# Two weight and activation tiles moved by 64 bytes each in a kernel of 32 graph blocks

## The chip, the cores and the metric

The kernel runs on one core of one Trainium2 chip, as one program in one launch. The metric is the device time of that program in microseconds; the median of three runs of the kernel before is 1295.74 us (1294.81 to 1297.44).

## The reference

32 graphs of 256 nodes with 256 features each (`x`), each with a dense 256 x 256 adjacency `adj`, pass through four blocks, each of them "layernorm of x plus block(x)":

- block 0: `relu(concat(x, adj @ x / deg) @ W.T)`;
- block 1: three graph convolutions, `adj @ (x @ Wi) + bi`, with relu after the first two;
- block 2: attention of 8 heads of 64 over the nodes: `qkv = x @ W_qkv`, `softmax(q @ k.T / 8) * 0.33 + 0.33 * adj + 0.33 * exp(-adj)` times `v`, then `@ W_out + b_out`, with a node mask;
- block 3: `scores = q @ k.T / 8` with a small `q` and `k` (64), a row sum of `scores * adj`, a softmax of that over the nodes, and its product with `x @ W_v.T`.

All of it is float32.

## The kernel before

One graph is one pass through all four blocks, and four or five graphs are in work at once. After a head (`first_graphs`) that fills this pipeline comes a loop of 28 equal slots (`slot(s)`, s from 5 to 32), in which each engine does the steps of graphs s-5 to s+1 in an order written out by hand, and then a tail (`last_graphs`). The order of the TensorE steps of a slot stands at L1834 to L1881.

To get float32 accuracy from the one-pass float32r products, each operand is kept in two tiles, a high part (`_h`) and a low part (`_l`); a product a @ b becomes a_h b_h + a_h b_l + a_l b_h. The helper `product` (L1506) issues these; `nodes_product` (L1532 on) issues a 256 x 256 by 256 x 256 product as 12 matmuls of 128 x 128 by 128 x 256, often cut in 8 that need only the high part of the late operand (`HI`) and 4 that need its low part (`LO`). In each matmul the left argument is the stationary operand, loaded into the array by a LDWEIGHTS of its own, and the right one is the moving operand. The trace names the moving operand first: `psum<-wout_h,oT_h` streams wout_h past the stationary oT_h.

The matmuls of a slot which read float32r tiles of 128 partitions, in their order, are these (moving x stationary tile, count):

- `hidden(0)` sup x w123, 8 then 4, with `tail_adj_k` (k3 x adjT, 8) between;
- four steps of transposes, two of scores, two of attend, `gate_row`;
- `support(1)` w123 x hidT, 12; `qk(2)` x2T x wqkv, 12; `support0 HI` w0 x fT, 8; `hidden(1)` adjT x sup, 12; `support0 LO` w0 x fT, 4; `self_product` w0 x fT, 12; `project_out` wout x oT, 24; `support(2)` w123 x hidT, 12; `values HI` wqkv x x2T, 8 of 512 columns; `gcn_out` sup x adjT, 12; `values LO`, 4 of 512 columns; `aggregate` sup x adjT, 12; `qk(3)` x2T x wqkv, 12;
- `gate_column`, transposes, scores, attend, `x3_transpose`;
- `qk(0)` x2T x wqkv, 12; `tail_project HI` w3 x x3T, 8 of 384 columns; `mix` adjT x fT, 12; `tail_project LO`, 4 of 384 columns; `qk(1)` x2T x wqkv, 12; and then the next slot's `hidden(0)`.

Every tile is a static buffer of each partition, placed by `sb()` right behind the one before it, at the next multiple of 32 bytes. Three unused buffers (`space_0`, `space_1` of 64 bytes, `space_2` of 32) and 16 unused elements in each row of `qkT` (`HALF` is 16 elements, 64 bytes) stand between tiles. With them every product of high and low parts has its two operands 64 bytes apart modulo 128.

What prints below are the function that allocates the tiles and the TensorE steps.

Of the kernel before, what the change touches and what calls it, by code (L numbers as in the profile page):

```python
# [13 lines left out]
def graph_blocks_kernel(nc, x_d, adj_d, nodemask, xT_d, adjT_d, w0_d, w123_d, L1_b1, L1_b2, L1_b3, wqkv_d, wout_d,  # L14
# [3 lines left out]
    P = 128  # L18
# [12 lines left out]
    HALF = 16  # L31
# [5 lines left out]
    with ctx:  # L37
        def sb(name, shape, dt=F32):
            return ctx.enter_context(nc.sbuf_tensor(name, shape, dt))
# [20 lines left out]

        w0 = [sb(f"w0_{s}", [P, FT, 2 * F], F32R) for s in "hl"]
        w123 = [sb(f"w123_{s}", [P, 3, FT, F], F32R) for s in "hl"]
        wqkv = [sb(f"wqkv_{s}", [P, FT, 3, INNER], F32R) for s in "hl"]
        wout = [sb(f"wout_{s}", [P, PAIRS, F], F32R) for s in "hl"]
        w3 = [sb(f"w3_{s}", [P, FT, L3C], F32R) for s in "hl"]

# [29 lines left out]
        x2_pre = sb("x2_pre", [P, NT, F])  # L96
        x2 = sb("x2", [P, NT, F])
        x2_bout = sb("x2_bout", [P, 2, NT, F])
        x2T = [sb(f"x2T_{s}", [P, FT, N], F32R) for s in "hl"]


        v_sb = sb("v_sb", [P, NT, INNER])
        w0_raw = v_sb
        qkT = [sb(f"qkT_{s}", [P, 2, 2, N + HALF], F32R)[:, :, :, 0:N] for s in "hl"]
# [2029 lines left out]
```

How the kernel before makes its waits and increments, by code:

```python
        def reuse(eng, semaphore, n):  # L239
            if n > 0:
                eng.wait_ge(semaphore, n)
# [7 lines left out]
        @block.sync  # L250
# [35 lines left out]
            def store(g):  # L286
                b = g % 2
                sp.wait_ge(act_y, once(g))
                sp.dma_start(out_d[bass.ds(g, 1)].rearrange("g p n f -> (g p) n f"), y_sb[:, b]) \
                    .then_inc(dma_out[b], 16)
# [28 lines left out]
            load_nodes(1)  # L319
            sp.dma_start(wqkv_raw[:, :, :], wqkv_d).then_inc(dma_wqkv, 16)
            sp.dma_start(wout_raw[:, :, :], wout_d).then_inc(dma_wout, 16)
            sp.dma_start(w3_raw[:, :, :], w3_d).then_inc(dma_w3, 16)
            for k in range(2, G + 6):
                if live(k):
                    load(k)
                if live(k - 6):
                    store(k - 6)
            for b in range(2):
                sp.wait_ge(dma_out[b], 16 * (G // 2))
# [1 line left out]
        @block.gpsimd  # L331
        def _(pool):
            nc.gpsimd.memset(one[:, :], 1.0)
            nc.gpsimd.memset(eps[:, :], LN_EPS)
            nc.gpsimd.memset(minus_half[:, :], -0.5).then_inc(pool_const, 1)
            nc.gpsimd.memset(ident[:, :], 0.0).then_inc(pool_ident, 1)
            pool.wait_ge(pool_ident, 1)
            nc.gpsimd.affine_select(out=ident[:, :], in_=ident[:, :], compare_op=ALU.not_equal, fill=1.0,
                                    base=0, pattern=[[-1, P]], channel_multiplier=1).then_inc(pool_ident, 1)
            pool.wait_ge(pool_const, 1)
```

## Time and profile before

| what | value |
|---|---|
| median of 3 runs | 1295.74 us |
| profiled execution, its own time | 1296.16 us |
| its span, first to last instruction | 1294.4 us |
| TensorE matmul busy | 1269.5 us, 98% |
| TensorE weight load busy | 1162.2 us, 90% |
| VectorE busy | 1160.8 us, 90% |
| ScalarE busy | 969.8 us, 75% |
| GpSimd busy | 179.3 us, 14% |
| DMA, mean | 38 GB/s |
| chain that ended last | TensorE 94% |
| granted TensorE clock | 0.998 |

Matmuls overlap, and the end of each is modelled: a row's length (0.28 us for 256 columns) is not what a matmul costs. What it costs is the distance from its start to the start of the next. In the views by time a row with xN is N matmuls of one form, and the second number is the time from the start of the first to the end of the last.

### The profile page before, as it was taken

The page shows a single profiled execution, that of the slowest core. Times are in us where ns is not written, and L with a number is a line of the kernel's source. Part 1 is how long each engine was busy: PE and PEld are TensorE (multiplying, and loading weights), DVE is VectorE, ACT ScalarE, POOL GpSimd, SP SyncE. Part 2 cuts the span into 40 slices and gives each one's busy share as a digit, 9 for nine tenths or more (in the row PEclk, how much of TensorE's full clock was granted, in tenths as well). Part 3 has the DMA queues.
Part 4 walks back from the last instruction along what each step waited for, and adds up shares of the span by engine and source line. Part 5 has one row for each costly group of instructions (what it writes and reads, how often), then busy time and mean ns, then how long its engine had stood idle before and what let it go on. Part 6 is the DMA issues. An engine that isn't in the chain of part 4 may idle for free.

```text
span 1294.4 us, 30393 instructions
## 1 busy us (share of the span) xinstructions
PE 1269.5 (98%) x10848; PEld 1162.2 (90%) x10848; DVE 1160.8 (90%) x3661; ACT 969.8 (75%) x2573; POOL 179.3 (14%) x393
## 2 busy tenths in 40 slices
PE   7999999999999999999999999999999999999996
PEld 7898899999999999999999999999999999999985
DVE  7988999999999999999999999999999999998984
ACT  7677777778778778778778777787777787777773
POOL 0100111101111101111101111101111111111101
PEclk9999999999999999999999999999999999999999
DMA  6110111110111110111110111100111100110000
GB/s 227 34 35 2 35 43 43 44 43 1 43 43 43 43 43 2 43 43 43 43 31 14 43 43 43 43 26 19 43 44 43 43 17 28 43 43 10 10 9 25
DMA packets 34309, 49.02 MB, mean 38 GB/s; under 512 B 7920, under 2 KB 16880, under 8 KB 34160
## 3 DMA queue, kind: packets, MB, share of 16 engines
q1 hardware_dynamic: 34160, 47.08, 11.5%
q8 instruction: 88, 1.44, 0.5%
q14 instruction: 61, 0.50, 0.1%
HBM read 38.68 MB, written 8.39 MB: 36 GB/s over the span
## 4 chain that ended last, share of the span: by engine, by line
PE 94%; ACT 2%; DVE 2%; DMA 1%; POOL 1%; issue 1%; SPq 0%; ACTq 0%; POOLq 0%; DVEq 0%
PE psum L1506 63%; PE psum L1520 11%; PE psum L1756 9%; PE psum L1714 8%; PE psum L1807 1%; PE psum L1810 1%; PE psum L1819 1%; ACT work L545 1%; DMA adjT_sb<-in_adjT 1%; PE psum L1830 0%; ACT x L597 0%; POOL rstd L349 0%; DVE bn L902 0%; DMA v_sb<-in_w 0%; DVE work L1080 0%
## 5 line engine op out<-in xcount | busy, mean ns | idle before, releaser
L545 ACT ACTIVATE work<-work,shift 128x256 f32<-128x256 f32 x512 | 253.2, 498 | 5.5 <-DVE shift L1061 5.5
L1080 DVE SCALAR_TENSOR_TENSOR work<-work,rsum,extra 128x256 f32<-128x256 f32 x512 | 217.0, 475 | 1.0
L396 ACT ACTIVATE work<-psum 128x512 f32<-128x512 f32 x256 | 138.1, 595 | 73.3 <-PE psum L1520 69.4
L1061 DVE CUSTOM_DVE_ANT_0 work<-psum,minus_big 128x256 f32<-128x256 f32 x512 | 189.5, 417 | 3.3 <-PE psum L1714 3.2
L346 POOL TENSOR_TENSOR mv<-mv,eps 128x2 f32<-128x2 f32 x128 | 31.0, 243 | 1094.4 <-DVE mv L923 1094.4
L396 ACT ACTIVATE sup_h<-psum 128x512 fp32r<-128x512 f32 x124 | 73.3, 591 | 117.8 <-PE psum L1506 117.5
L1506 PE MATMUL psum<-x2T_h,wqkv_h 128*128 128x256 f32 x512 | 145.7, 285 | 0.0
L1506 PE MATMUL psum<-x2T_l,wqkv_h 128*128 128x256 f32 x512 | 143.0, 279 | 0.0
L1506 PE MATMUL psum<-x2T_h,wqkv_l 128*128 128x256 f32 x512 | 142.8, 279 | 0.0
L1520 PE MATMUL psum<-ident,work 128*128 128x128 f32 x1024 | 129.0, 274 | 0.0
L1756 PE MATMUL psum<-work,v_sb 128*64 128x256 f32 x1024 | 124.7, 385 | 1.0 <-ACT work L396 1.0
L396 ACT ACTIVATE qkT_h<-psum 128x512 fp32r<-128x512 f32 x128 | 75.3, 589 | 55.9 <-PE psum L1506 55.7
L1520 PEld LDWEIGHTS psum<-ident,work 128*128 128x128 f32 x1024 | 113.0, 141 | 1.4 <-DVE work L1080 0.6
L349 POOL TENSOR_TENSOR rstd<-mv,minus_half 128x2 f32<-128x2 f32 x128 | 106.9, 835 | 10.0
L1756 PEld LDWEIGHTS psum<-work,v_sb 128*64 128x64 f32 x1024 | 67.9, 136 | 37.4 <-ACT work L396 1.4
L873 DVE TENSOR_TENSOR sup_l<-psum,sup_h 128x512 fp32r<-128x512 f32 x124 | 85.0, 686 | 14.4 <-ACT sup_h L396 14.2
L545 ACT ACTIVATION_READ_ACCUMULATOR work<-work,shift 128x1 f32 x512 | 97.3, 190 | 0.0
L1506 PEld LDWEIGHTS psum<-x2T_h,wqkv_h 128*128 128x128 f32 x512 | 96.5, 188 | 0.5 <-DVE x2T_l L873 0.2
L1506 PEld LDWEIGHTS psum<-x2T_l,wqkv_h 128*128 128x128 f32 x512 | 96.8, 189 | 0.0
L1506 PEld LDWEIGHTS psum<-x2T_h,wqkv_l 128*128 128x128 f32 x512 | 96.3, 188 | 0.0
L902 DVE BATCH_NORM_STATS2 bn<-x_pre 128x6 f32<-128x256 f32 x256 | 94.9, 414 | 0.3
L873 DVE TENSOR_TENSOR qkT_l<-psum,qkT_h 128x512 fp32r<-128x512 f32 x128 | 86.6, 678 | 3.0 <-ACT qkT_h L396 3.0
(185 smaller groups left out, 3794.3 us busy)
## 6 DMA issues: line engine op xcount, KB each, us to landing
xT_sb<-in_xT SPq DMA_DIRECT2D x32, 256.0 KB, 2.6
adjT_sb<-in_adjT SPq DMA_DIRECT2D x32, 256.0 KB, 2.9
adj_sb<-in_adj SPq DMA_DIRECT2D x32, 256.0 KB, 4.5
x_sb<-in_x SPq DMA_DIRECT2D x32, 256.0 KB, 4.7
out<-y_sb SPq DMA_DIRECT2D x32, 256.0 KB, 4.5
work<-in_wqkv SPq DMA_DIRECT2D x1, 1536.0 KB, 10.5
mask_row<-in_nodemask SPq DMA_DIRECT2D x32, 32.0 KB, 4.5
w_raw<-in_w SPq DMA_DIRECT2D x3, 256.0 KB, 5.7
```

The lines of the kernel that those rows point to most:

```text
L346: nc.gpsimd.tensor_tensor(mv[:, k, :, 1], mv[:, k, :, 1], eps[:, :], ALU.add) \
L349: nc.gpsimd.tensor_tensor(rstd[:, k], mv[:, k, :, 1], minus_half[:, :], ALU.pow) \
L396: return nc.scalar.activation(dst, src, ACT.Copy, scale=scale)
L545: last = nc.scalar.activation(prob[:, p % 2, i, h], prob[:, p % 2, i, h], ACT.Exp, bias=shift[:, p % 2, h, i:i + 1], scale=-1.0, accum_out ...
L873: return V_.tensor_tensor(dst, src, f32(hi_part), ALU.subtract)
L902: last = V_.bn_stats(out=bn[:, k, t], in_=src[:, t])
L1061: last = V_.tensor_tensor_reduce(out=prob[:, p % 2, i, h], in0=bank(SCORES[p] + h)[:, i * N:(i + 1) * N], in1=minus_big[:, g % 2, i], scal ...
L1080: last = V_.scalar_tensor_tensor(out=prob[:, p % 2, i, h], in0=prob[:, p % 2, i, h], scalar=rsum[:, p % 2, h, i:i + 1], in1=extra[:, g % 2 ...
L1506: last = mm(dst, left, right, start=opens and n == 0, stop=closes and n == len(steps) - 1)
L1520: last = nc.tensor.transpose(dst[:, r * N + t * P:r * N + (t + 1) * P], src[:, t, block_of(r)], ident[:, :])
L1714: last = mm(bank(SCORES[p] + h)[:, i * N:(i + 1) * N], qkT[left][rows, p % 2, 0, block_of(i)], qkT[right][rows, p % 2, 1], start=n == 0 an ...
L1756: last = mm(bank(PV[p])[h * D:(h + 1) * D, 0:N], v_sb[:, k, (2 * p + h) * D:(2 * p + h + 1) * D], probT[:, p % 2, h, k], start=k == 0, sto ...
```

## The change

Four buffers of 64 bytes that nobody reads or writes are added to the allocation. No instruction is added, removed or moved; addresses alone change.

```
         w123 = [sb(f"w123_{s}", [P, 3, FT, F], F32R) for s in "hl"]
+        sb("space_3", [P, HALF])
         wqkv = [sb(f"wqkv_{s}", [P, FT, 3, INNER], F32R) for s in "hl"]
+        sb("space_4", [P, HALF])
         wout = [sb(f"wout_{s}", [P, PAIRS, F], F32R) for s in "hl"]
...
         x2_bout = sb("x2_bout", [P, 2, NT, F])
+        sb("space_5", [P, HALF])
         x2T = [sb(f"x2T_{s}", [P, FT, N], F32R) for s in "hl"]
 
 
+        sb("space_6", [P, HALF])
         v_sb = sb("v_sb", [P, NT, INNER])
```

`wqkv` moves up by 64 bytes, what lies behind it up to `x2_bout` by 128, `x2T` by 192, and `v_sb` and all behind it by 256. Modulo 128 only `wqkv` and `x2T` change. Modulo 256 others do too. The first byte of each tile (of its high part; the low part has the same remainder), as the sizes in the allocation add up:

| tile | before | before mod 128 | after mod 128 | before mod 256 | after mod 256 |
|---|---|---|---|---|---|
| w0, w123 | 41760, 49952 | 32 | 32 | 32 | 32 |
| wqkv | 62240 | 32 | 96 | 32 | 96 |
| wout, w3 | 86816, 95008 | 32 | 32 | 32 | 160 |
| adjT | 132256 | 32 | 32 | 160 | 32 |
| fT, sup, hidT | 148704, 152800, 167136 | 96 | 96 | 224 | 96 |
| x2T | 179424 | 96 | 32 | 224 | 160 |
| oT, x3T, k3 | 196448, 208736, 215904 | 96 | 96 | 96 | 96 |

All pieces that a matmul reads begin a multiple of 512 bytes behind the tile's first byte, so the remainders hold for each of them. The address of the stationary operand less that of the moving one, modulo 256, is:

| product | before | after |
|---|---|---|
| support(1), support(2), support0, self_product, values | 192 | 64 |
| qk, hidden(0), tail_adj_k, project_out, tail_project | 64 | 192 |
| hidden(1), mix | 64 | 64 |
| gcn_out, aggregate | 192 | 192 |

## Rows read from the trace of the kernel before

**Rows 1.** Page, busy time of each engine.
```profile
PE 1269.5 (98%) x10848; PEld 1162.2 (90%) x10848; DVE 1160.8 (90%) x3661; ACT 969.8 (75%) x2573; POOL 179.3 (14%) x393
```

**Rows 2.** Busy time by stretch: one slot, 27 slots (clock is the last but two).
```profile
540.16:579.23 39.07, 39.07 (x339) 35.92 (x337) 35.97 (x115) 29.96 (x80) 5.69 (x12) 1.00 0.11 36
149.51:1204.31 1054.80, 1054.80 (x9074) 969.80 (x9073) 970.24 (x3077) 809.11 (x2160) 153.51 (x324) 1.00 0.11 35
```

**Rows 3.** By time, TensorE in one slot: start, length, work; first of each step.
```profile
548.16 0.28 PE L1506 MATMUL psum<-w_l,hidT_h 128*128 128x256 f32 x1
...
549.45 0.28 PE L1506 MATMUL psum<-x2T_h,wqkv_h 128*128 128x256 f32 x1
...
550.87 0.28 PE L1506 MATMUL psum<-w_h,fT_h 128*128 128x256 f32 x1
...
551.81 0.28 PE L1506 MATMUL psum<-adjT_h,sup_h 128*128 128x256 f32 x1
...
553.18 0.63 PE L1506 MATMUL psum<-w_h,fT_l 128*128 128x256 f32 x4
553.65 0.28 PE L1506 MATMUL psum<-w_h,fT_h 128*128 128x256 f32 x1
...
555.06 0.28 PE L1506 MATMUL psum<-wout_h,oT_h 128*128 128x256 f32 x1
...
557.78 0.28 PE L1506 MATMUL psum<-w_h,hidT_h 128*128 128x256 f32 x1
...
559.14 0.39 PE L1506 MATMUL psum<-wqkv_h,x2T_h 128*128 128x512 f32 x1
...
560.97 0.28 PE L1506 MATMUL psum<-sup_h,adjT_h 128*128 128x256 f32 x1
...
562.38 1.09 PE L1506 MATMUL psum<-wqkv_h,x2T_l 128*128 128x512 f32 x4
563.31 0.30 PE L1506 MATMUL psum<-sup_h,adjT_h 128*128 128x256 f32 x1
...
564.74 0.28 PE L1506 MATMUL psum<-x2T_h,wqkv_h 128*128 128x256 f32 x1
...
566.01 0.28 PE L1506 MATMUL psum<-x2T_h,wqkv_l 128*128 128x256 f32 x1
```

**Rows 4.** The same view, the last steps of that slot.
```profile
572.83 0.28 PE L1506 MATMUL psum<-x2T_l,wqkv_h 128*128 128x256 f32 x1
...
573.99 0.28 PE L1506 MATMUL psum<-x2T_h,wqkv_l 128*128 128x256 f32 x1
574.20 0.44 PE L1506 MATMUL psum<-w_h,x3T_h 128*128 128x384 f32 x1
...
575.70 0.28 PE L1506 MATMUL psum<-adjT_h,fT_h 128*128 128x256 f32 x1
...
577.12 0.86 PE L1506 MATMUL psum<-w_h,x3T_l 128*128 128x384 f32 x4
577.81 0.28 PE L1506 MATMUL psum<-x2T_h,wqkv_h 128*128 128x256 f32 x1
```

**Rows 5.** By time, ScalarE in that slot: the step that tail_project waits for.
```profile
573.57 0.58 ACT L396 ACTIVATE x3T_h<-psum 128x512 fp32r<-128x512 f32 x1
```

**Rows 6.** By time, TensorE in the slot that begins at 1008.95 us.
```profile
1018.25 0.29 PE L1506 MATMUL psum<-x2T_h,wqkv_h 128*128 128x256 f32 x1
...
1019.63 0.28 PE L1506 MATMUL psum<-w_h,fT_h 128*128 128x256 f32 x1
...
1020.54 0.28 PE L1506 MATMUL psum<-adjT_h,sup_h 128*128 128x256 f32 x1
...
1021.95 0.64 PE L1506 MATMUL psum<-w_h,fT_l 128*128 128x256 f32 x4
```

**Rows 7.** Page, costliest groups: two evictions, to tiles with different first bytes.
```profile
L396 ACT ACTIVATE sup_h<-psum 128x512 fp32r<-128x512 f32 x124 | 73.3, 591 | 117.8 <-PE psum L1506 117.5
L396 ACT ACTIVATE qkT_h<-psum 128x512 fp32r<-128x512 f32 x128 | 75.3, 589 | 55.9 <-PE psum L1506 55.7
```

More of the change, by code:

```diff
@@ L62, in graph_blocks_kernel @@
         w123 = [sb(f"w123_{s}", [P, 3, FT, F], F32R) for s in "hl"]
+        sb("space_3", [P, HALF])
         wqkv = [sb(f"wqkv_{s}", [P, FT, 3, INNER], F32R) for s in "hl"]
+        sb("space_4", [P, HALF])
         wout = [sb(f"wout_{s}", [P, PAIRS, F], F32R) for s in "hl"]
@@ L98, in graph_blocks_kernel @@
         x2_bout = sb("x2_bout", [P, 2, NT, F])
+        sb("space_5", [P, HALF])
         x2T = [sb(f"x2T_{s}", [P, FT, N], F32R) for s in "hl"]
+        sb("space_6", [P, HALF])
         v_sb = sb("v_sb", [P, NT, INNER])
```

## The prediction

> **What bounds the kernel now.** I read the page first: TensorE is busy 98% of the span, its weight loads and VectorE 90% each [rows 1]. Then the busy time by stretch: 27 slots take 1054.80 us, 39.07 each, TensorE has no idle time in them, and its clock is at the full level, 2.4 GHz [rows 2]. So the kernel is TensorE's slot, 28 times, with a head and a tail of 200 us together (1294.4 less 28 x 39.07). A change of 0.01 us in the slot is 0.28 us in the time; the 0.2% that a measurement here can tell from no change is 2.6 us, or 0.093 us a slot.
>
> Then I read the slot by time, and looked only at starts. The same matmul of 128 x 128 by 256 columns has two paces. `project_out` issues 24 from 555.06 to 557.78, 113.3 ns each, and `support(2)` 12 in 1.36 us, also 113.3; `self_product` takes 1.41 us for its 12 (117.5), `gcn_out` 1.41, `mix` 1.42, `qk(1)` 1.42 up to the next slot at 579.23 [rows 2 to 4]. The four together give 117.9 ns; I use 117.8. The difference is 4.5 ns a matmul. The same tiles are slow at one place and fast at another: w123 past hidT takes 117.3 in `support(1)` (11 in 1.29 us) and 113.3 in `support(2)` [rows 3]. The pace is therefore not fixed by the operands alone; it is something that is entered and left at certain places, and then kept. The slots repeat, so what one shows stands for nearly all [rows 2].
>
> **How the pace goes with addresses.** I set the paces of rows 3, 4 and 6 beside the table of remainders and found three regularities. They are fitted to this trace, not known.
> (a) Left: when the moving operand's first byte jumps modulo 256 at a seam, a quick stretch ends. `hidden(1)` (moving 160) is followed by `support0 LO` (moving 32), and the 4 matmuls there take 0.47 us, 117.5 each, after 1.37 us for 12 before them [rows 3]. In the slot at 1008.95 `support0 HI` is fast (8 in 0.91) and the `hidden(1)` behind it is slow (12 in 1.41) [rows 6]. From `values HI` (moving 32) to `gcn_out` (moving 224) the same. Where it doesn't jump, fast stays fast: `project_out` to `support(2)`, both 32.
> (b) Entered: only inside products whose stationary operand lies 64 above the moving one modulo 256, and there when the product before had 192 or wasn't of this kind: `hidden(1)` after `support0 HI` (1.37 for 12, so about 0.01 until it is fast), `project_out` after `self_product`, `qk(3)` after `aggregate` (11 in 1.27, 115.5 mean), `qk(0)` after transposes (10 in 1.16, 116) [rows 3, 4].
> (c) Products with 192 never get fast by themselves: `gcn_out`, `aggregate`, `self_product`, `support(1)`. `mix` and `qk(1)`, behind the 384-column `tail_project` with the same 64, stay slow too.
> Modulo 128 these don't come out: `hidden(1)` to `support0 LO` is no jump there.
>
> **The change, step by step.** It adds no instruction, wait, semaphore or transfer, and four unused buffers. The diff moves remainders, also those of wout, w3, adjT, fT, sup and hidT modulo 256. Per slot, by (a) to (c):
> - `support(1)`: distance 192 to 64, behind `gate_row`'s transposes, like `qk(0)` now: from 117.3 to 116 over its 12: -0.02 us.
> - `qk(2)`: 64 to 192, moving jumps: slow as now (1.42): 0.
> - `support0 HI`: distance now 64, behind 192: enters. 0.94 to 0.92: -0.02.
> - `hidden(1)`: no jump in front any more (32 after 32): 1.37 to 1.36: -0.01.
> - `support0 LO`, `self_product`: moving 32 still, no jump: stay fast. 0.47 to 0.45 and 1.41 to 1.36: -0.07.
> - `project_out`: moving jumps to 160, distance 192: 24 slow. 2.72 to 2.82: +0.10.
> - `support(2)`: jumps back, distance 64: enters like `hidden(1)`: 1.36 to 1.37: +0.01.
> - `values HI`: moving jumps from 32 to 96. The 512-column matmul takes 228.8 ns at the fast pace (8 in 1.83 us) and 232.5 at the slow one (`values LO`, 4 in 0.93) [rows 3]: 8 x 3.7 = +0.03.
> - `gcn_out`: 192, no jump, slow as now: 0. `values LO`: distance 64, enters: -0.01. `aggregate`: 0.
> - `qk(3)`: 64 to 192, slow throughout: 1.27 for 11 becomes 1.30, and one ns or so at the seam, where the operands of both products now coincide modulo 128: +0.04.
> - `qk(0)`: slow throughout, +0.02, but it ends at 574.1 and `tail_project` starts at 574.20, behind ScalarE's x3T_h, which runs from 573.57 to 574.15 [rows 4, 5]. That wait of 0.1 us hides it; were it gone, 0.02 a slot are 0.6 us.
> - `tail_project`: distance 64 to 192 with 384 columns, which no row shows. Below, its present 0.69 us for 4 against a 384-column share of the fast pace is a gain of 0.01 at best; above, the 3.7 ns of the 512-column case over 12 is 0.05. I take +0.01, near the lower end, as it isn't clearly fast now.
> - `mix`: jumps to 32 with distance 64, now behind 192, so it enters: 1.42 to 1.38: -0.04.
> - `hidden(0)` and `tail_adj_k`: 64 to 192. `hidden(0)` is slow already. `tail_adj_k` is 8 short ones: between -0.01 and +0.03, taken as 0.
> - `qk(1)`: slow as now.
> - The evictions and weight preparations that write moved tiles: sup_h, first byte 224, takes 591 ns, and qkT_h, whose halves start at 224 and 32, takes 589 [rows 7]: 0, within 2 ns of 0.6 us either way. VectorE at 35.97 of 39.07 us a slot [rows 2] leaves room.
> Transposes, scores and attend keep their distances or, x2 and x3 against the identity, change by 128 or not at all; 0, with a bound of 0.03 either way.
> Sum: -0.02 -0.02 -0.01 -0.07 +0.10 +0.01 +0.03 -0.01 +0.04 +0.01 -0.04 = +0.02 us a slot, and 28 x 0.02 = 0.6 us. Head and tail, where TensorE also waits, are taken as 0, between -0.5 and +0.5. The profiled execution's own time of 1296.16 (its span is 1294.4) becomes 1296.8; it stands 0.4 above the median of 1295.74, so for a median I forecast 1296.3.
>
> **A rule against any effect.** Both paces exist on one and the same pair of tiles [rows 3], so something other than arithmetic slows one. The Trainium skill, "TensorE: Matmul & The Clock Gate", section on what happens when you issue a matmul, says that TensorE has two independent read ports and that loading the next tile's weights takes no bandwidth from the running matmul; "SBUF — State Buffer", section on who interferes with whom, says that TensorE never waits on anyone. By that rule, the change would be worth 0. Its issue gap for 256 columns, 109 ns, is shorter than both paces of this trace, so something the page leaves out is at work.
>
> **The rivals.**
> 1. *The pace has nothing to do with addresses.* It would be set by what each step waits for. For it: the same tiles at both paces. Against: a jump and a change of pace fall together too often. Time: the median again, 1295.7.
> 2. *Only the seams modulo 128 count* (a next weight load 0 bytes from the running moving operand), and that is what the change thins out: 8 such seams a slot now, 3 after (`support(2)` to `values HI`, `aggregate` to `qk(3)`, `qk(1)` to `hidden(0)`). Then `qk(2)`, `support0 HI`, `hidden(1)` and `qk(1)` run at the fast pace (-0.05 -0.03 -0.01 -0.05), and with nothing to end it `support0 LO` and `self_product` as well (-0.07), against +0.03 for `values HI` and +0.04 for `qk(3)`: -0.14 a slot, -3.9 us, 1291.9; half of it, without the last gain, -1.9 us. For it: `qk(2)` and `qk(1)`, slow today, both stand behind such a seam, and `qk(3)` and `qk(0)`, fast, don't. Against: `hidden(1)` to `support0 LO`, slow behind a 64 seam.
> 3. *The losses come and the entries don't* (slower). (a) holds, and a distance of 64 isn't enough to enter. At `project_out` the quick stretch of 36 matmuls that runs through `support(2)` breaks: +0.10 and 12 x 4.5 = +0.05, then `values HI` +0.03, `qk(3)` +0.04, and `hidden(1)`, which enters today, stays slow, +0.05: +0.27 a slot, +7.6 us, 1303.3. It decides from the point where fewer than about half of the entries (`support0 HI`, `support(2)`, `mix`) come: +0.13 a slot, 1299.4.
> 4. Other mixtures, such as a `gcn_out` that keeps a fast pace which `values` got into (-0.05 a slot), or scores that fall into the other pace: within 3 us of the median on either side.
>
> **How the numbers follow.** Forecast 0.45 (own range 1294.0 to 1298.8: ten uncertain terms of about 0.03 a slot add to 0.09 at worst); rival 1 0.12; rival 2 0.18; rival 3 0.15; the rest 0.10. Faster by over 0.2%: 0.12 from rival 2, 0.07 from the forecast's edge, 0.04 from the rest, 0.23. Slower: 0.15 from rival 3, 0.07 and 0.05, 0.27. Within: 0.50. The range reaches to rival 2's full time and into rival 3's half, 1291.8 to 1301.0.
>
> **What would show it.** In the slot by time after: `project_out` about 2.82 us from its first start to `support(2)`'s, `self_product` 1.36, `support0 HI` 0.92, `qk(2)` 1.42 still, `qk(3)` 1.30 for 11, `mix` 1.38, and the slot 39.09. A fast `qk(2)` and `qk(1)` speak for rival 2; unchanged numbers everywhere for rival 1; a slow `self_product` and `support(2)` for rival 3. The forecast is wrong if the slot is off by more than 0.09 us, and its reason is wrong if `project_out` stays at 2.72.

## The result, and the profile after

The change makes the kernel slower: 1303.62 us, median of 6 runs (1302.29 to 1304.27), against 1296.03 (1294.81 to 1297.44, 6 runs), ratio 1.0055, 95% interval 1.0042 to 1.0068. The forecast was 1296.3 in a range up to 1301.0; the time lies outside it, where the third rival (1303.3) had put it.

Page of the changed kernel, busy time of each engine:

```profile
PE 1276.3 (98%) x10848; PEld 1169.0 (90%) x10848; DVE 1160.7 (89%) x3661; ACT 970.5 (75%) x2573; POOL 179.0 (14%) x393
```

Its busy time by stretch (columns as in [rows 2]): one slot, all 27, and one slot that differs.

```profile
542.65:581.96 39.31, 39.31 (x339) 36.15 (x337) 35.95 (x115) 29.97 (x80) 5.68 (x12) 1.00 0.12 36
149.51:1210.78 1061.27, 1061.27 (x9075) 976.04 (x9073) 970.04 (x3077) 809.35 (x2160) 153.23 (x324) 1.00 0.11 35
739.21:778.32 39.11, 39.11 (x339) 35.96 (x337) 35.95 (x115) 29.94 (x80) 5.67 (x12) 1.00 0.11 36
```

The span grew from 1294.4 to 1301.0 us, and 27 slots from 1054.80 to 1061.27 [rows 2]: 6.47 of the 6.6 us, 0.24 a slot. TensorE still has no idle time there, its clock is as before, and VectorE and ScalarE do their work in the same time. The whole loss is TensorE's pace.

TensorE by time in the ordinary slot at 542.65, the first row of each step, as in [rows 3, 4]:

```profile
551.94 0.28 PE L1510 MATMUL psum<-x2T_h,wqkv_h 128*128 128x256 f32 x1
...
553.36 0.28 PE L1510 MATMUL psum<-w_h,fT_h 128*128 128x256 f32 x1
...
554.30 0.28 PE L1510 MATMUL psum<-adjT_h,sup_h 128*128 128x256 f32 x1
...
555.72 0.64 PE L1510 MATMUL psum<-w_h,fT_l 128*128 128x256 f32 x4
556.19 0.28 PE L1510 MATMUL psum<-w_h,fT_h 128*128 128x256 f32 x1
...
557.60 0.28 PE L1510 MATMUL psum<-wout_h,oT_h 128*128 128x256 f32 x1
...
560.43 0.28 PE L1510 MATMUL psum<-w_h,hidT_h 128*128 128x256 f32 x1
...
561.84 0.39 PE L1510 MATMUL psum<-wqkv_h,x2T_h 128*128 128x512 f32 x1
...
563.71 0.28 PE L1510 MATMUL psum<-sup_h,adjT_h 128*128 128x256 f32 x1
...
567.50 0.28 PE L1510 MATMUL psum<-x2T_h,wqkv_h 128*128 128x256 f32 x1
...
568.79 0.28 PE L1510 MATMUL psum<-x2T_h,wqkv_l 128*128 128x256 f32 x1
...
578.49 0.28 PE L1510 MATMUL psum<-adjT_h,fT_h 128*128 128x256 f32 x1
...
579.90 0.86 PE L1510 MATMUL psum<-w_h,x3T_l 128*128 128x384 f32 x4
580.60 0.28 PE L1510 MATMUL psum<-x2T_h,wqkv_h 128*128 128x256 f32 x1
...
581.96 0.28 PE L1510 MATMUL psum<-sup_h,w_h 128*128 128x256 f32 x1
```

Read from start to start: `project_out` takes 2.83 us (forecast 2.82, before 2.72), `values HI` 1.87, `qk(3)` 1.29 for 11. `hidden(1)` is slow at 1.42 (before 1.37), `self_product` 1.41 (forecast 1.36), `support(2)` 1.41 (forecast 1.37), `mix` 1.41 (forecast 1.38). `qk(1)` is quick, 1.36, and was to stay slow.

The slot at 739.21, of the same execution, took 39.11 us. Its rows:

```profile
749.92 0.28 PE L1510 MATMUL psum<-w_h,fT_h 128*128 128x256 f32 x1
...
750.84 0.28 PE L1510 MATMUL psum<-adjT_h,sup_h 128*128 128x256 f32 x1
...
752.20 0.62 PE L1510 MATMUL psum<-w_h,fT_l 128*128 128x256 f32 x4
...
754.01 0.28 PE L1510 MATMUL psum<-wout_h,oT_h 128*128 128x256 f32 x1
...
756.84 0.28 PE L1510 MATMUL psum<-w_h,hidT_h 128*128 128x256 f32 x1
...
758.21 0.39 PE L1510 MATMUL psum<-wqkv_h,x2T_h 128*128 128x512 f32 x1
```

This is nearly the forecast slot: `support0 HI` 0.92, `hidden(1)` 1.36, `support0 LO` with `self_product` 1.81 (slow: 1.88), `project_out` 2.83, `support(2)` 1.37. It came once in the 27. The addresses allow the forecast; they don't bring it about. It is also the slot that tests the exit at `project_out`: in the ordinary slot nothing quick stands in front of it, and it takes 2.83 us in both.

### The profile page after: what moved, and what is told of

Its sections match the earlier page's. It is cut to its first block, busy times and chain, and to the rows that moved or that the text cites. A ratio compares the mean times of both kernels' runs of the same rounds, so it can differ in the third digit from the quotient of the medians.

```text
span 1301.0 us, 30393 instructions
## 1 busy us (share of the span) xinstructions
PE 1276.3 (98%) x10848; PEld 1169.0 (90%) x10848; DVE 1160.7 (89%) x3661; ACT 970.5 (75%) x2573; POOL 179.0 (14%) x393
## 4 chain that ended last, share of the span: by engine, by line
PE 93%; DVE 2%; ACT 2%; DMA 1%; issue 1%; POOL 1%; SPq 0%; ACTq 0%; POOLq 0%; DVEq 0%
PE psum L1510 63%; PE psum L1524 11%; PE psum L1760 9%; PE psum L1718 8%; PE psum L1811 1%; PE psum L1814 1%; PE psum L1823 1%; ACT work L549 1%; DMA adjT_sb<-in_adjT 1%; PE psum L1834 0%; ACT x L601 0%; DVE work L1084 0%; POOL rstd L353 0%; DVE bn L906 0%; DVE work L1065 0%
```

## The experiments

A stretch is a row of matmuls at one pace, quick (113.3 ns for 256 columns) or slow (117.8 ns); a seam is where one product ends and the next begins; the jump is what the moving operand's first byte changes by there, modulo 256; the distance is that of the two operands, as in the table of remainders. Two theories run through the experiments. *Theory A*: leaving and entering the quick pace both go by the addresses modulo 256, as the forecast had it. *Theory P*: leaving goes by addresses, but whether a stretch enters is settled by the nanoseconds at which it meets a seam. The first runs were made before P was formed. Slot lengths and times of steps are means over the slots of each profile.

**TensorE alone.** Nothing but float32r matmuls of 256 columns between transposes, every other engine idle, for 16 distances and several jumps.

> Leaves the whole computation out: TensorE alone issues float32r matmuls (128 x 128 by 256 columns) from one buffer, with all other engines idle; its time says nothing, its starts do. 32 stretches of 24 with the stationary operand 0 to 496 bytes above the moving one modulo 512, in steps of 16, then 16 stretches with distances 64 and 192 at other first bytes, then pairs of stretches with a jump of the moving operand by 0, 64, 128 or 192. If the pace is a matter of the two read addresses: 113.3 ns near 64 modulo 128, more than 118 near 0, and the same at D and D + 256 (theory of remainders modulo 256) or at D and D + 128 (modulo 128). Both paces, 113.3 and 117.8, should appear at 64 or 192. If addresses have nothing to do with it, all stretches show one pace.

Four stretches of 24 matmuls by time; the first has distance 0, the next two distance 64 and the same addresses and the same four transposes in front, the last distance 192:

```profile
29.89 3.11 PE L400 MATMUL psum<-buf 128*128 128x256 f32 x24
...
43.02 3.08 PE L400 MATMUL psum<-buf 128*128 128x256 f32 x24
...
134.95 2.99 PE L400 MATMUL psum<-buf 128*128 128x256 f32 x24
...
138.13 2.97 PE L400 MATMUL psum<-buf 128*128 128x256 f32 x24
```

3.08 and 2.99 us for identical work are the two paces, settled at 117.8 and 113.3 ns, at a granted clock of 1.00 throughout. Both exist with no other engine at work, so neither comes from one. Over the last 15 gaps of each stretch, distances 0, 32, 112, 128 and 144 give 120.0, 118.4, 120.0, 118.7 and 120.1 ns; 113.3 occurred at 64 and 192 alone, and there in 5 of 20 stretches. Adding 256 to a distance changes nothing (0 and 256 120.0; 112 and 368 120.0), adding 128 does (0 and 128). The distance counts modulo 256.

**Which jumps end a quick stretch.**

> TensorE alone, nothing else at work; the layer's computation is left out. Each trial is three transposes (some with a preamble of products before them), 8 products at distance 192, 14 at distance 64 (and 8 more at 192 where the trial starts the jump from there), then 14 products whose moving operand begins 0, 64, 128 or 192 bytes further modulo 256 and whose distance is 64 or 192. Theory A (a quick stretch of 113.3 ns ends where the moving operand's first byte changes modulo 256, except by +64 from 64 to 192): the 14 behind a jump of 128 or 192 take 117.8 each in every trial that came in quick, the ones behind no jump 113.3, the ones at +64 113.3 only if the distance goes 64 to 192. Theory B (it is a matter of chance at each seam, by the phase in which the seam is met): both paces turn up in repeats of the same jump, in the same proportion for all jumps. Entry: theory A from the first such run says that distance 192 to 64 with no jump enters in about 3 of 4, any other jump in 1 of 4 or fewer; theory B gives the same share for every jump.

Counts over both kernels, for stretches that came in quick: the distance alone changed and no jump of the moving operand, 35 of 35 kept; +64 into distance 192, 8 of 8 kept; +64 into distance 64, 0 of 9; +128, 0 of 15; +192, 0 of 14. Between products of 256 columns leaving goes by addresses, here without exception. Entering doesn't: behind a slow stretch at distance 192, with no jump, distance 64 entered in 30 of 44; at the other seams into distance 64 in 7 of 17; at seams into 192 in 0 of 28. And (c) falls: right behind transposes, 9 of 48 stretches at distance 192 were quick from the start. The same 16 matmuls (2 at distance 192, then 14 at 64) of two trials of one execution that are alike up to there, by time:

```profile
49.28 1.98 PE L296 MATMUL psum<-buf 128*128 128x256 f32 x16
62.66 2.05 PE L296 MATMUL psum<-buf 128*128 128x256 f32 x16
```

**The swap modulo 128 alone, and the move modulo 128 not at all.** `e_swap_only` makes the swap and keeps every distance modulo 256; `e_mod128_same` swaps nothing, and moves wout to x2T by 128.

```
+        sb("space_3", [P, 16])      # e_swap_only: ahead of wqkv
+        sb("space_4", [P, 48])      #   ahead of wout
+        sb("space_5", [P, 16])      #   ahead of x2T
+        sb("space_6", [P, 48])      #   ahead of v_sb
+        sb("space_4", [P, 32])      # e_mod128_same: ahead of wout
+        sb("space_6", [P, 32])      #   ahead of v_sb
```

> wqkv +64, x2T +320 (64 modulo 256), all others moved by a multiple of 256: only the swap modulo 128, with the distance in qk and values kept modulo 256. If the swap costs: 1301 to 1303. If remainders modulo 256 of the others do: 1296 within 2, and with fewer seams at distance 0 perhaps 1294.

> wqkv stays, wout to x2_bout and x2T move by 128, v_sb and all behind by 256: nothing changes modulo 128, and modulo 256 the same tiles move as in the change except wqkv and x2T. If the loss comes from remainders modulo 256 (project_out, support(2) and hidden(1) at the slow pace): about +0.17 us a slot, 1301. If it comes from the swap of wqkv and x2T modulo 128: as before, 1296.

The swap: 1295.9 us, ratio 0.9999 (0.9989 to 1.0008), slot 39.02. The move without the swap: 1300.1, ratio 1.0031 (1.0018 to 1.0044), slot 39.17. The second rival and the thought that seams count modulo 128 fall.

The trace of the swap shows more. Two slots next to each other, by time from `qk(2)` to `support0 LO`:

```profile
315.81 0.28 PE L1510 MATMUL psum<-x2T_h,wqkv_h 128*128 128x256 f32 x1
...
317.19 0.28 PE L1510 MATMUL psum<-w_h,fT_h 128*128 128x256 f32 x1
...
318.10 0.28 PE L1510 MATMUL psum<-adjT_h,sup_h 128*128 128x256 f32 x1
...
319.51 0.64 PE L1510 MATMUL psum<-w_h,fT_l 128*128 128x256 f32 x4
```

```profile
354.82 0.28 PE L1510 MATMUL psum<-x2T_h,wqkv_h 128*128 128x256 f32 x1
...
356.24 0.28 PE L1510 MATMUL psum<-w_h,fT_h 128*128 128x256 f32 x1
...
357.18 0.28 PE L1510 MATMUL psum<-adjT_h,sup_h 128*128 128x256 f32 x1
...
358.55 0.63 PE L1510 MATMUL psum<-w_h,fT_l 128*128 128x256 f32 x4
```

`qk(2)` takes 1.38 us in one and 1.42 in the next; of the 27 slots it is quick in 14, and `hidden(1)` in the 13 others. One program, one execution, the same addresses: already this shows that addresses alone don't settle an entry. And `gcn_out` is quick in all 27, from its first matmul on, behind the 512 columns of `values HI` and a jump of +128:

```profile
561.50 0.28 PE L1510 MATMUL psum<-sup_h,adjT_h 128*128 128x256 f32 x1
...
562.86 1.10 PE L1510 MATMUL psum<-wqkv_h,x2T_l 128*128 128x512 f32 x4
```

That is 1.36 us for 12, so the count of exits above doesn't hold behind a product of 512 columns; whether the pace was kept there or entered at once is not shown. In the move without the swap, `support0 HI` to `self_product` are quick, at the remainders that they have in the change too, where they are slow; its loss is `project_out` +0.11, `qk(3)` +0.04 and `values HI` +0.03.

**wqkv and x2T as in the change, the rest as before.**

```
+        sb("space_3", [P, 16])      # ahead of wqkv
+        sb("space_4", [P, 48])      #   ahead of wout
+        sb("space_5", [P, 48])      #   ahead of x2T
+        sb("space_6", [P, 16])      #   ahead of v_sb
```

> wqkv +64, x2T +448 (192 modulo 256), all others moved by a multiple of 256: wqkv and x2T exactly as in the change modulo 256, everything else as before. With the run before it this divides the change's loss in two: its excess over 1296 is the part of wqkv and x2T (qk at distance 192: 1297 by the theory of remainders modulo 256, qk(3) and values +0.07 a slot gives 1298), the other run's the part of the rest.

1300.65 us, ratio 1.0041 (1.0026 to 1.0056), slot 39.17, where theory A gave 1298. `qk(3)` and `values HI` cost 0.06 together (expected 0.07), and `hidden(1)` lost its pace (+0.04), though its own addresses and those of the product in front are those of the kernel before.

**wout and w3: moved alone, and alone not moved.** `e_wout_only` adds to the kernel before two spacers; `e_after_wout_back` is the change with only wout and w3 back at 32 modulo 256, written as five spacers in the kernel before.

```
+        sb("space_3", [P, 32])      # e_wout_only: ahead of wout
+        sb("space_4", [P, 32])      #   ahead of adjT
+        sb("space_3", [P, 16])      # e_after_wout_back: ahead of wqkv
+        sb("space_4", [P, 48])      #   ahead of wout
+        sb("space_5", [P, 32])      #   ahead of adjT
+        sb("space_6", [P, 16])      #   ahead of x2T
+        sb("space_7", [P, 16])      #   ahead of v_sb
```

> One part of the change alone: only wout and w3 move by 128 bytes, from 32 to 160 modulo 256; everything else has the remainders of before. project_out then has distance 192 in place of 64 and its moving operand jumps by 128 in front and behind. Theory A: project_out +0.10 us, support(2) behind it slow or entering again, +0.01 to +0.05, tail_project within 0.02: slot +0.11 to +0.17, time 1299.2 to 1300.8. Theory P: project_out's loss is not sure, as a product at distance 192 can be quick too if it gets in (in the change its 24 were slow); hidden(1) and the rest can shift with it, slot between -0.05 and +0.2. Rival from the result of the change with wout back (1293.7): the loss of the change is wout's alone, then 1303.

> The change, but wout and w3 go back to 32 modulo 256, so that project_out has its distance of 64 and self_product to project_out is no jump of the moving operand. Theory A (the loss of project_out comes from its own remainders): project_out is back at 2.72 us for 24, support(2) behind it at 1.36, together -0.16 us a slot against the change, time 1299.1; what is left of the loss is that of wqkv and x2T. Rival (the loss belongs to what comes before, self_product or support0, whose quick stretch is no more): project_out stays at 2.80 or above and the time within 1.5 us of the change's 1303.6.

Moved alone: 1300.55 us, ratio 1.0019 (1.0008 to 1.003; the kernel before took 1298.14 us beside it), slot 39.18, so +0.11. Put back: 1293.68, ratio 0.9972 (0.9962 to 0.9981), slot 38.93: faster than the kernel before, and 0.38 a slot faster than the change, where `project_out` and `support(2)` were to give 0.16. Busy time of its 27 slots, then `support0 HI` to `values HI` by time:

```profile
150.51:1201.54 1051.03, 1051.03 (x9074) 965.99 (x9073) 969.71 (x3077) 808.93 (x2160) 153.40 (x324) 1.00 0.11 35
```

```profile
550.43 0.28 PE L1511 MATMUL psum<-w_h,fT_h 128*128 128x256 f32 x1
...
551.35 0.28 PE L1511 MATMUL psum<-adjT_h,sup_h 128*128 128x256 f32 x1
...
552.71 0.62 PE L1511 MATMUL psum<-w_h,fT_l 128*128 128x256 f32 x4
...
554.52 0.28 PE L1511 MATMUL psum<-wout_h,oT_h 128*128 128x256 f32 x1
...
557.24 0.28 PE L1511 MATMUL psum<-w_h,hidT_h 128*128 128x256 f32 x1
...
558.60 0.39 PE L1511 MATMUL psum<-wqkv_h,x2T_h 128*128 128x512 f32 x1
```

`support0 HI`, `hidden(1)`, `support0 LO` and `self_product`, all ahead of `project_out` and at the same remainders as in the change, are quick here. The parts don't add: wout +0.11, all the rest -0.14, both +0.24 a slot. That led to theory P: what wout and w3 alter reaches the steps in front of `project_out` by way of the next slot, as a shift in time. The shift is argued, not measured.

**The same addresses, another moment.** One matmul a slot is added ahead of `support(1)`, of which nothing is used; its result is overwritten.

```
+                if part == HI and layer == 1:
+                    mm(bank(SUP[layer])[:, 0:64], cut(hidT_of(g), A, 0, block_of(0))[0],
+                       w123[0][:, layer][A, 0, 0:64], start=True, stop=True)
```

> The change, with one matmul more a slot: support(1) begins with a product of its own first weights by 32 columns, whose result the next matmul overwrites. No address moves. Theory P (which pace a stretch gets into is settled by the nanoseconds at which it meets a seam; only leaving goes by the addresses): the stretch behind it may fall into the quick pace at qk(2), support0 HI or hidden(1) (then 8 in 0.91 us, hidden(1) 12 in 1.36, self_product 1.36), and the slot is 39.31 + 0.04 - 0.15 = 39.20 us; at least one of the two lengths, 32 and 64 columns, does so. Theory A (entries go by the addresses): both leave all paces of the change as they are, slot 39.31 plus the matmul itself, 39.34 to 39.42.

> The same with 64 columns. Theory P: another moment at the seams, so the paces may differ from those of the change and of the 32 columns at the same addresses. Theory A: all as in the change, slot 39.34 to 39.42 us.

> The kernel before with the 64-column matmul ahead of support(1), no address moved. Theory P: hidden(1), quick today in 26 of 28 slots, can lose its pace (+0.04 us), or support0 HI and qk(2) can get it. Theory A: all paces as before, slot 39.07 plus the matmul itself, 39.10 to 39.18.

`support(1)` grows by 0.11 in the first and the third; in the second by 0.09, as its last seven matmuls are quick. With 32 columns the change's slot is 39.22 all the same, not 39.42: `support0 HI` -0.03, `hidden(1)` -0.05, `support0 LO` with `self_product` -0.07, `support(2)` -0.04. With 64 it is 39.10: in addition `aggregate` and `qk(3)`, -0.10, in 26 of 27 slots. In the kernel before, `hidden(1)` lost its pace (+0.04), and `qk(2)` and `support0 HI` gained it (-0.07): slot 39.16. The entries move though no address does, the exits (`project_out` at 2.83 us, behind a quick `self_product` in both forms of the change) stay. The times, of one execution each: 1301.22, 1297.85 and 1299.79 us, with 1298.14 for the kernel before beside them, so the slots are the better measure.

A smaller form of the matmul was timed over more executions, and both forms once more:

```
+                    mm(bank(SUP[layer])[0:32, 0:32], cut(hidT_of(g), A, 0, slice(0, 32))[0],
+                       w123[0][:, layer][A, 0, 0:32], start=True, stop=True)
```

> The change with one matmul more a slot ahead of support(1), now with 32 columns of weights by 32 columns, so that it costs less itself (some 0.03 to 0.06 us by the 28 ns between the records of gate_row and support(1); 0.11 with 128 columns of weights). No address moves. Theory P (phase): the seams are met at another moment, and the stretch from support0 HI to self_product may fall into the quick pace, as it did with the 32- and the 64-column matmul: slot 39.30 + 0.04 - 0.12 = 39.22 us or, with aggregate and qk(3) as well, 39.10; time 1297.5 to 1301.5. Theory A (addresses alone) or an unlucky phase: 1304.3 to 1305.5.

> The change with the small matmul, once more and unaltered, for its trace: of its five executions one took 1298.6 us and four 1305.7 to 1308.7. Theory P: the one program has two outcomes, settled by where the seams are first met, so a trace of a long one shows, at the same addresses and the same instructions, the stretch from support0 HI to self_product slow (self_product 1.41 us against 1.36 in the short one) and a slot of 39.3 to 39.4 us against 39.08. Theory A: the paces of the steps are the same in both, and the 8 us lie somewhere else (the head, a wait, the clock).

> The change with the 64-column matmul, which has been seen in one execution only (1297.9 us, slot 39.10). Theory P: its executions fall in two groups too, near 1298 and near 1306, or in the first alone. Theory A: 1306 to 1307, and the 1297.9 is not seen again.

`e_after_small` took 1298.56 us in its profiled execution and 1305.67 to 1308.68 in the other four; `e_small_again`, the same program, 1308.48 (profiled) and 1306.01. Median 1305.93, ratio 1.0076 (1.0061 to 1.0092). The two traces, 27 slots each:

```profile
151.32:1206.42 1055.10, 1055.10 (x9101) 969.88 (x9100) 968.77 (x3077) 810.15 (x2160) 153.51 (x324) 1.00 0.11 35
```

```profile
150.34:1214.68 1064.34, 1064.34 (x9101) 978.93 (x9100) 970.42 (x3077) 809.41 (x2160) 153.23 (x324) 1.00 0.11 35
```

One program, one clock, one count of instructions: 39.08 and 39.42 us a slot. In either trace the slots agree within 0.01 us, but for one of 39.14 in the first. `support0 HI`, `self_product` and `project_out` begin, in the short and in the long one:

```profile
552.85 0.28 PE L1510 MATMUL psum<-w_h,fT_h 128*128 128x256 f32 x1
...
555.58 0.28 PE L1510 MATMUL psum<-w_h,fT_h 128*128 128x256 f32 x1
...
556.94 0.28 PE L1510 MATMUL psum<-wout_h,oT_h 128*128 128x256 f32 x1
```

```profile
555.36 0.28 PE L1510 MATMUL psum<-w_h,fT_h 128*128 128x256 f32 x1
...
558.18 0.28 PE L1510 MATMUL psum<-w_h,fT_h 128*128 128x256 f32 x1
...
559.60 0.28 PE L1510 MATMUL psum<-wout_h,oT_h 128*128 128x256 f32 x1
```

`self_product` takes 1.36 us in one and 1.42 in the other. Theory A can't have this. The two traces are of two chips, but the five executions of `e_after_small`, on one chip, had both times. These two executions keep what they fell into from slot to slot; that each slot hands the next the same shift would explain it, but no run measures such a shift, and the trace of `e_swap_only` changes from slot to slot. The 64-column form gave, in four executions, 1300.33 to 1303.18 (ratio 1.0043, 1.0026 to 1.006), slot 39.17: the first 1297.85 (slot 39.10) was the best of its five, and my two groups near 1298 and 1306 were not what came. `aggregate` and `qk(3)`, quick in 26 slots of the first trace, are quick in none of this one.

**Layouts with two classes of address.** Weights and adjT at 32 modulo 256, all activation tiles of the products at 96 (`e_two_classes`) or at 224 (`e_two_classes_neg`).

```
+        sb("space_3", [P, 32])      # e_two_classes: ahead of adjT
+        sb("space_4", [P, 32])      #   ahead of v_sb
+        sb("space_3", [P, 32])      # e_two_classes_neg: ahead of adjT
+        sb("space_4", [P, 32])      #   ahead of fT
+        sb("space_5", [P, 32])      #   ahead of oT
```

> The kernel before with two spacers more: every weight and adjT begin at 32 modulo 256, every activation tile of the products at 96. Products that move a weight have distance 64, products that move an activation 192, and the moving operand jumps only by 64 or 192. Theory A (exits at jumps; +64 from distance 64 to 192 keeps the pace, the way back at +192 is the open point): if the way back keeps it too, all of hidden, support, self_product, project_out, values, gcn_out run at 113.3 or 228.8, the slot is about 38.80 us against 39.07 and the time 1288 to 1290; if the way back ends it, the products with 192 behind a quick one are quick and those after them slow, slot 39.0 to 39.15, time 1294 to 1298. Theory B (chance): slot within 0.05 of before. Rival: only the number of different remainders matters, with two of them it is faster than before by at least 0.1 us a slot.

> The same with the activation tiles at 224 modulo 256: products that move a weight have distance 192, those that move an activation 64. Theory A: products with 192 don't become quick by themselves, so project_out, hidden(1), support(2) and values stay at 117.8 (+0.10, +0.04, +0.05, +0.03), while gcn_out, aggregate and self_product, now at 64, may enter (-0.05 each): slot 39.05 to 39.20, time 1295 to 1300. If the sign of the distance doesn't matter, the slot is that of the two classes with 96 within 0.03 us.

> The two-class layout with 224 once more, in five rounds, for its time beside both kernels: 1292.4 again, ratio 0.9955 to 0.9973. If its gain of 0.20 us a slot were a matter of luck at the start of an execution, it would come out with some executions near 1296.

With 96: 1295.46 us, ratio 0.999 (0.998 to 0.9999), slot 39.00. With 224: 1292.41, ratio 0.9964 (0.9951 to 0.9977); again, in 11 executions, 1293.11 (1291.42 to 1295.25), ratio 0.9977 (0.9968 to 0.9986), slots 38.87 and 38.91. It beats both kernels. My reason for it was wrong: `project_out`, `hidden(1)`, `support(2)` and `values`, at distance 192, were to stay slow, and all ran quick: `qk(2)` (distance 64) entered, its step to `support0 HI` is the +64 that keeps the pace, and no jump follows up to `values`. The expectation also put `self_product` at 64; it is at 192. In the first trace `aggregate` and `qk(3)` are quick in 25 of 27 slots, in the second in 8.

**The small matmul in that layout**, ahead of `support(1)` and ahead of `mix`.

> The best layout so far (activations at 224 modulo 256, all weights and adjT at 32) with the same small matmul. Theory P: support(1) and qk(2) can be quick as well (-0.02, -0.03), or the stretch from support0 HI can be lost (+0.15): slot 38.87 + 0.04, between -0.05 and +0.15. Theory A: slot 38.90 to 38.93, no pace changed.

> The best layout so far with the small matmul ahead of mix. Slow there are mix (0.94 and 0.47), qk(1) (1.41) and hidden(0) HI (0.94), together 0.14 us above the quick pace. Theory P: some of them become quick: slot 38.87 + 0.04 - 0.05 to -0.14, time 1289.5 to 1292; an unlucky phase leaves them, 1293.5. Theory A: 1293.5.

1297.14 us in one execution (slot 39.03), and 1296.35, ratio 1.0003 (0.9994 to 1.0012), slot 39.03. The matmul itself cost 0.11 in both instead of the 0.04 that I had allowed, and neither changed the pace of `mix`, `qk(1)` or `support(1)`. What the slot grew by beyond it, up to 0.05, is `aggregate` and `qk(3)`, quick in 5 of 27 slots. As that differs by as much between the two traces without the matmul, these two speak for neither theory.

## Why the prediction was wrong

The reading of the bound held: the loss is the slot's, 28 times, with no other engine in it. Step by step:

- **(a), left: the exit is right between products of 256 columns, with one exception; the terms came out for other reasons.** `project_out` +0.11 (forecast +0.10), `values HI` +0.03 (+0.03), `qk(3)` +0.04 (+0.04). The jumps of +64 into distance 192 keep the pace, which the forecast didn't separate. In the ordinary slot no quick stretch reached `project_out` or `qk(3)`: they didn't enter, rather than leave, which costs the same. The +0.03 of `values HI` isn't its jump: it takes 1.86 us in `e_mod128_same` and `e_two_classes`, at distance 64 with no jump and a quick `support(2)` in front, and 1.84 in `e_swap_only`, with the change's jump and distance 192. In all layouts here it takes 1.83 to 1.84 at 192 and 1.86 at 64.
- **(b), entered: the step that failed.** "`support0 HI`: distance now 64, behind 192: enters" was worth -0.02 and came to 0.00; "`support0 LO`, `self_product` ... stay fast", -0.07, came to 0.00; "`hidden(1)`: no jump in front any more", -0.01, came to +0.04; "`support(2)` ... enters like `hidden(1)`", +0.01, came to +0.05; "`mix` ... enters", -0.04, came to 0.00; `support(1)`, -0.02, to 0.00. Together 0.24 us a slot above the forecast, as much as the whole loss; all other terms together missed by -0.02. What the runs show in its place: distance and product in front only allow an entry. In the trace of before almost all slots repeat the same outcome, so 27 slots are close to one observation; I read a place where entering happened as a rule that makes it happen. The places where it did were four cases, not a hundred, and the trace had counterexamples: `qk(2)`, at distance 64 behind 192, stayed slow in all but one slot, and in that one [rows 6] `qk(2)` and `support0 HI` are quick and `hidden(1)` slow, at the same addresses.
- **(c): wrong.** "`qk(1)`: slow as now" came to -0.05, quick at distance 192. It runs so in `e_after_x` too (1.37 us).
- **What no step had.** `scores(2)` +0.03, at the end of its bound, and `aggregate` +0.02, put at 0; `qk(0)` and the wait behind it, 0 by the forecast, gave 0.03 back, and `tail_project`, forecast at +0.01, 0.01. Evictions and head and tail: 0, as said (0.1 us of the 6.6 lie outside the 27 slots).
- **Rivals.** The third named the outcome (losses come, entries don't) and, at +0.27 a slot against +0.24, its size. Its reason, that a distance of 64 isn't enough to enter, is right, but not that the entries don't come: `support0 HI` and `support(2)` enter at the change's own addresses in the slot at 739.21 and with the added matmul. Rival 2 is refuted by `e_swap_only`; its 8 seams before are 7 by the table of remainders. Rival 1's "what each step waits for" is wrong as put, for no wait is involved, yet "the same tiles at both paces" was the better half of the truth.

The Trainium skill, "TensorE: Matmul & The Clock Gate", section on what happens when you issue a matmul, says that loading the next weights takes no read bandwidth from the running matmul. With TensorE alone at work, the same 256-column matmuls cost 113.3 to 120.1 ns by distance, and 113.3 or 117.8 at one distance, so something between the operands' addresses counts; whether it is the weight load's reads is not shown. "SBUF — State Buffer", section on who interferes with whom, says that PE never waits on anyone; nothing here speaks against it, as both paces are there with the other engines idle.

Left open: what settles an entry. That it isn't the addresses alone is shown, by both paces at the same addresses within one program; that it is the moment, theory P, fits but is not shown, since no run sets the moment by itself, and what it would be a moment of (an offset between weight loads and moving reads, say) isn't shown either. Open too is why the change keeps to one outcome in six executions while `e_after_small` has two.

## What to carry to other kernels

A loop whose slots repeat the same outcome gives little more than one observation of each seam, however many slots there are; before a pattern from it becomes a rule, a kernel with TensorE alone tells what goes by the addresses and what doesn't. Where a kernel is bound by back-to-back float32r matmuls, the layout was worth from 0.4% less to 0.6% more time here, but only whole layouts can be compared: the price of one moved tile (wout: +0.11 or +0.38 us a slot, by what else had moved) is not a property of the tile. And such a variant is judged over several executions, as one program here took 1298.6 or 1305.7 to 1308.7 us.

## What the runs showed of the hardware that was not expected

- Float32r matmuls of 128 x 128 by 256 columns, back to back, issue every 113.3 or 117.8 ns at a distance of 64 or 192 bytes modulo 256 between stationary and moving operand, and every 116.6 to 120.1 ns at the 14 other distances tried, with nothing else running.
- The quick pace holds on until something ends it: between products of 256 columns, 35 of 35 quick stretches outlived a seam where only the distance changed, and none of 38 a jump of +128, +192 or, into distance 64, of +64.
- At the same addresses, in one execution, `qk(2)` was quick in 14 slots of 27 and slow in 13 (`e_swap_only`); one program took 39.08 or 39.42 us a slot in two executions (`e_after_small`, `e_small_again`).
- With 512 columns, eight matmuls took 1.83 to 1.84 us at distance 192 and 1.86 at 64 in every layout, whatever the pace in front.
- A 32-column matmul added to a slot made it 0.09 us shorter (39.31 to 39.22), though it costs 0.11 itself.
